# A graph network on one core: last edges looked up in a column of copied node rows, the dense moments spread over more turns, and more state gathers at a seam of the tail

## What is computed

```python
    def _L0_gnn_ref(x, edge_index, edge_bias, Wq, bq, Wk, bk, Wv, bv, Wo, bo):
...
        attn = jnp.einsum('ehd,ehd->eh', q_i, k_j) * scale + edge_bias
        seg_max = jax.ops.segment_max(attn, col, num_segments=N)
...
        out = jax.ops.segment_sum(weighted_v, col, num_segments=N)
...
    def _L1_gnn_ref(x, edge_index, edge_type, edge_emb_W, msg_W, msg_b, upd_W, upd_b, ln_g, ln_b):
...
        m = jax.nn.relu(m_in @ msg_W.T + msg_b)
        agg = jax.ops.segment_sum(m, dst, num_segments=x.shape[0])
...
    def _L3_gnn_ref(x, hyperedge_index, hyperedge_weight, W1, b1, gamma, beta, W2, b2):
...
        h = _hconv(x, W1, b1, node_idx, edge_idx, hyperedge_weight)
        mu = h.mean(axis=0)
        var = h.var(axis=0)
        h = gamma * (h - mu) * jax.lax.rsqrt(var + EPS) + beta
        return _hconv(h, W2, b2, node_idx, edge_idx, hyperedge_weight)
```

## Time and profile before

| | us |
|---|---|
| median of 3 runs | 2510.71 (2508.42 to 2510.8) |
| the profiled execution | 2507.46, of which the span from first to last instruction is 2505.7 |
| GpSimd busy | 1776.4 (71% of the span), 1419 instructions |
| VectorE busy | 1579.2 (63%) |
| TensorE busy | 1393.9 (56%) |
| ScalarE busy | 861.4 (34%) |
| mean granted TensorE clock | 0.772 of full speed |

### The profile page before, as it was taken

One profiled execution on the slowest core, in us unless ns is written; L12 is line 12 of the kernel. 1 busy time (PEld: TensorE's weight loads), 2 busy tenths in 40 slices (PEclk: granted clock), 3 DMA queues, 4 the chain that ended last, 5 costly groups with the idle time before them and its releaser, 6 DMA issues. The chain is left out here.

```text
span 2505.7 us, 21855 instructions
## 1 busy us (share of the span) xinstructions
PE 1393.9 (56%) x4580; PEld 725.9 (29%) x4580; DVE 1579.2 (63%) x4917; ACT 861.4 (34%) x1813; POOL 1776.4 (71%) x1419
## 2 busy tenths in 40 slices
PE   6778488888546666547888366354555640011121
PEld 1444244444313333213433244122223330001110
DVE  8889378878727989949899454243444464534443
ACT  0111156667515767735877211011112320000000
POOL 5774677777078888148787587788757878777887
PEclk8899699999768887768999687677777865555555
DMA  1111244444254566344666577567796863323331
GB/s 25 25 33 41 76 110 123 123 123 113 57 113 115 142 162 152 100 99 105 145 147 137 121 203 200 138 171 194 158 228 163 245 181 81 86 63 72 72 72 43
DMA packets 358128, 297.94 MB, mean 119 GB/s; under 512 B 110941, under 2 KB 312428, under 8 KB 357981
## 3 DMA queue, kind: packets, MB, share of 16 engines
q1 hardware_dynamic: 260397, 225.43, 33.4%
q0 software_dynamic: 97600, 71.11, 14.7%
HBM read 199.75 MB, written 96.70 MB: 118 GB/s over the span
## 5 line engine op out<-in xcount | busy, mean ns | idle before, releaser
L2219 DVE TENSOR_TENSOR_SCAN tl_S<-tl_same,tl_S,tl_pX 128x500 f32<-128x500 bf16 x96 | 120.3, 1253 | 317.6 <-issue 219.1
L2108 PE MATMUL tl_pX<-k_ident,tl_ga 125*128 125x125 f32 x400 | 84.6, 349 | 421.1 <-DMA tl_ga<-table_TE,k_s_idxE 321.8
L481 POOL DMA_INDIRECT tl_ga<-table_TE,k_s_idxE x200 | 243.0, 1215 | 63.4 <-issue 58.5
L2108 PEld LDWEIGHTS tl_pX<-k_ident,tl_ga 125*128 125x128 f32 x400 | 57.6, 178 | 437.0 <-DMA tl_ga<-table_TE,k_s_idxE 331.4
L481 POOL DMA_INDIRECT ms_ga<-table_T,k_idxS x100 | 143.4, 1434 | 36.1 <-issue 29.6
L481 POOL DMA_INDIRECT tl_ga<-table_TH,k_send x100 | 123.1, 1231 | 51.7 <-issue 51.1
L1288 PE MATMUL tl_pCon<-dr_BC,dn_cT 128*128 128x512 f32 x196 | 130.6, 754 | 51.2 <-DVE dr_o L1307 21.6
L283 POOL DMA_INDIRECT table_ptab<-k_ef,ix_scatI x100 | 124.8, 1248 | 47.9 <-issue 47.9
L481 POOL DMA_INDIRECT at_ga<-x,k_src x100 | 126.5, 1265 | 44.7 <-issue 27.3
L481 POOL DMA_INDIRECT at_gb<-xw,at_dstI x100 | 128.9, 1289 | 35.5 <-issue 29.0
L481 POOL DMA_INDIRECT eq_ga<-table_T,k_idxS x100 | 126.1, 1261 | 35.0 <-issue 30.0
(11 more groups left out here) (469 smaller groups left out, 4363.9 us busy)
## 6 DMA issues: line engine op xcount, KB each, us to landing
dr_x<-x SPq DMA_DIRECT2D x97, 256.0 KB
result<-dr_o SPq DMA_DIRECT2D x97, 256.0 KB
dm_xT<-xT SPq DMA_DIRECT2D x32, 768.0 KB
tl_fac<-table_dinv SPq DMA_DIRECT2D x50, 250.0 KB
table_T<-at_y SPq DMA_DIRECT2D x50, 224.0 KB
table_T<-ms_y SPq DMA_DIRECT2D x50, 224.0 KB
table_T<-eq_y SPq DMA_DIRECT2D x50, 224.0 KB
table_TE<-tl_y SPq DMA_DIRECT2D x50, 224.0 KB
```

The source lines that it names most:

```text
L481: nc.gpsimd.indirect_dma_start(out=buf[:, k, :], out_offset=None, in_=table, in_offset=bass.IndirectOffsetOnAxis(ap=index[:, CT * c + k:CT ...
L2108: last = nc.tensor.transpose(pX[j % 2][:, k * TP:(k + 1) * TP], ga[j % RG][:, k, :], K["ident"][0:TP, 0:TP])
L2219: nc.vector.tensor_tensor_scan(S[i][:], same[j % RM][:], pX[i][:, 0:CE], 0.0 if j % NC == 0 else S[1 - i][:, CE - 1:CE], ALU.mult, ALU.add ...
```

## The change

Six edits in one step.

1. **A table of node rows takes the place of `ptab`.** The input `xw` gets `E` in its column 129. SP copies the whole of it, 50000 rows of 132 numbers (26.4 MB), to a table `XW` in HBM, in 5 pieces, where it copied 195.3 KB. The 100 scatters of last edges write into column 129 of `XW`, and wait for the whole copy.
2. **No lookups.** Attention gathers its source rows from `XW` in place of `x` (528 bytes a row in place of 512), so the last edge comes with the row; `biased` copies it to `K["pq"]`. The 100 gathers of `pq` in index, attention and message phases go, and with them the message phase's `source_rows` (three small vector instructions a turn). One `source_rows` over all chunks stands at the end of attention.
3. **Moments in attention**: one group a turn and two in two turns of eight, in place of three in three turns of four (`AT_QUADS`); 3 supers, 24 turns, in place of 5 supers in 20. Squares come in three turns of eight.
4. **Moments with messages**: three groups in each of 24 turns (8 supers), transposes and keeping of one super beside the first groups of the next, with two PSUM banks.
5. **Records**: 13 chunks with messages (every second turn), 12 in the equivariant phase, in place of 6 and 19.
6. **The tail's seam**: 8 chunks of state gathers (`WIDE_SEAM`) after the second pass and 13 between its chunks, in place of 4 and 17. In the second half of the second pass one dense group a turn in place of two; the 12 groups that this leaves over (`dense_seam`) stand between the second and the third pass.

```diff
             for name in ("ident", "identb", "heads", "cols"):
                 sp.dma_start(K[name][:], g[name]).then_inc(s_in, 16)
-            sp.dma_start(T["ptab"].rearrange("(a b) c -> a (b c)", a=16), g["ptab0"].rearrange("(a b) c -> a (b c)", a=16)).then_inc(s_tab, 16)
+            for i in range(PIECES):
+                n = N // PIECES
+                sp.dma_start(T["XW"][n * i * DW:n * (i + 1) * DW, :].rearrange("(a b) o -> a (b o)", a=400),
+                             g["xw"][n * i:n * (i + 1), :].rearrange("(a b) c -> a (b c)", a=400)).then_inc(s_tab, 16)
...
-            pool.wait_ge(s_tab, 16)
+            pool.wait_ge(s_tab, 16 * PIECES)
             pool.wait_ge(s_ends_idx, 1)
             for t in range(NT):
                 nc.gpsimd.indirect_dma_start(
-                    out=T["ptab"], out_offset=bass.IndirectOffsetOnAxis(ap=scatI[:, t:t + 1], axis=0),
-                    in_=K["ef"][:, t:t + 1], in_offset=None, bounds_check=N - 1, oob_is_err=False).then_inc(s_scat, 16)
+                    out=T["XW"], out_offset=bass.IndirectOffsetOnAxis(ap=scatI[:, t:t + 1], axis=0),
+                    in_=K["ef"][:, t:t + 1], in_offset=None, bounds_check=N * DW - 1, oob_is_err=False).then_inc(s_scat, 16)
             pool.wait_ge(s_scat, 16 * NT)
-            for t in range(CT * PQ):
-                nc.gpsimd.indirect_dma_start(out=K["pq"][:, t:t + 1], out_offset=None, in_=T["ptab"],
-                                             in_offset=bass.IndirectOffsetOnAxis(ap=src[:, t:t + 1], axis=0)).then_inc(s_gat, 16)
...
-                gathers(pool, s_ga[c % RA], K["src"], c, g["x"], ga[c % RA])
+                gathers(pool, s_ga[c % RA], K["src"], c, T["XW"].rearrange("(n c) o -> n (c o)", c=DW), ga[c % RA])
...
-                    if s < MA:
-                        dn.moments(pe, s)
+                    if s < 8 * AT_SUPERS:
+                        dn.moments(pe, s // 8, range(AT_QUADS[s % 8], AT_QUADS[s % 8 + 1]))
+                        if s % 8 == 7:
+                            dn.turn_moments(pe, s // 8)
                     out(s)
...
-                nc.vector.tensor_tensor(z[c % 3][:, CT:2 * CT, :], ga[c % RA][:], bc(bo, CT), ALU.add).then_inc(s_z2, 1)
+                nc.vector.tensor_copy(K["pq"][:, CT * c:CT * c + CT], ga[c % RA][:, :, D + 1])
+                nc.vector.tensor_tensor(z[c % 3][:, CT:2 * CT, :], ga[c % RA][:, :, 0:D], bc(bo, CT), ALU.add).then_inc(s_z2, 1)
...
-                if live(s + 3 + PQA):
-                    last_edges(s + 3 + PQA)
-                if 0 <= s - 14 < SLOTS:
-                    records(s - 14)
+                if s >= 0 and s % 2 == 0 and s // 2 < SLOTS:
+                    records(s // 2)
...
-                    dn.moments(pe, MA + s)
+                    if s > 0 and s % 3 == 0:
+                        dn.turn_moments(pe, AT_SUPERS + s // 3 - 1)
+                    if dn.ms_part(s) is not None:
+                        dn.moments(pe, AT_SUPERS + s // 3, range(3 * (s % 3), 3 * (s % 3) + 3))
...
+AT_QUADS = (0, 2, 3, 4, 5, 6, 7, 9, 9)
+AT_PARTS = (0, 2, 5)
...
             for c in range(NC):
                 fetch(J_NODE + c)
-                if c + SEAM < NC - SEAM:
+                if c + SEAM < NC - WIDE_SEAM:
                     keep_states(c + SEAM)
-            for c in range(NC - SEAM, NC):
+            for c in range(NC - WIDE_SEAM, NC):
                 keep_states(c)
             stored(pool, J_EDGE)
...
                 if t == J_EDGE:
                     batch_norm()
+                    for d in dense_seam():
+                        dn.combine(dve, d)
```

More of the change, by code:

```diff
@@ L43 @@
 RING = 4
-PQ = 6
-PQA = 10
-SLOTS = 6
+SLOTS = 13
+PIECES = 5
 class Chain:
@@ L1121, in flatten, with moments @@
-    def flatten(self, act, j):
-        h = j // 4
-        if j >= MT or j % 4 < 3:
-            return
+    def moments(self, pe, h, quads):
+        nc, pS = self.nc, self.bank_of(h)
+        count = min(PACK, DQ - PACK * h)
+        for k in quads:
+            if k >= count:
+                return
+            n = 3 * h + k // 3
+            a, b = self.span(n)
+            u = 512 * (k % 3)
+            w = min(512, b - a - u)
+            if k % 3 == 0:
+                pe.wait_ge(self.s_xT[n % 2], 16 * (n // 2 + 1))
+                pe.wait_ge(self.s_z2, n + 1)
+            if k == 0:
+                need(pe, self.s_kept, h + 1 - len(self.pS))
+            at = PW - NV - NV * k
+            nc.tensor.matmul(pS[0:PW, 0:w], self.Vx[:, at:at + PW], self.xT[:, n % 2, u:u + w], start=k == 0, stop=False)
+            last = nc.tensor.matmul(pS[0:PW, 0:w], self.Vz[:, at:at + PW], self.z2[:, n % 2, u:u + w], start=False, stop=k == count - 1)
+            if k % 3 == 2 or k == count - 1:
+                last.then_inc(self.s_mom, 1)
@@ L1126, in flatten, with turn_moments @@
+    def turn_moments(self, pe, h):
+        pe.wait_ge(self.s_flat, h + 1)
+        for i in range(4):
+            last = self.nc.tensor.transpose(self.bank_of(h)[:, i * PW:(i + 1) * PW], self.flat[:, i * 128:(i + 1) * 128], self.K["ident"][0:PW, 0:PW])
+        last.then_inc(self.s_mT, 1)
+    def flatten(self, act, h):
         act.wait_ge(self.s_mom, 3 * h + 3)
         need(act, self.s_mT, h)
-        self.nc.scalar.activation(self.flat[:], self.pS[0:PW, :], ACT.Identity, bias=self.off[:]).then_inc(self.s_flat, 1)
@@ L1332, in message_phase @@
         pA, pM, pO, pR = (a.ps(n, [128, 512]) for n in ("pA", "pM", "pO", "pR"))
-        dn.pS = a.ps("pS", [128, 512])
-        miss = a.sb("miss", [TP, CT])
-        s_pq = [a.sem(f"last_edges{i}") for i in range(2)]
-        s_idx, s_miss, s_rec = a.sem("source_rows"), a.sem("miss"), a.sem("records")
+        dn.pS = [a.ps(f"pS{i}", [128, 512]) for i in range(2)]
+        s_rec = a.sem("records")
         (s_w, s_eps, s_kind, s_tw, s_tA, s_xs, s_oneh, s_psM, s_m, s_S, s_psO,
@@ L1901, in _, with first, dense_seam @@
                 dn.coefficients(dve, s)
+SEAM, WIDE_SEAM, SEAM_ROWS = 4, 8, 12
+KEPT = 2 * NC - SEAM - WIDE_SEAM
 def dense_turn(t):
-    first = [min(DQ, u if u < NC else min(2 * u - NC, u + NC)) for u in (t, t + 1)]
-    return range(first[0], first[1])
+    def first(u):
+        if u <= NC:
+            return u
+        if u <= KEPT:
+            return 2 * u - NC
+        return min(DQ, u + KEPT - NC + (SEAM_ROWS if u > 2 * NC else 0))
+    return range(first(t) + (SEAM_ROWS if t == 2 * NC else 0), first(t + 1))
+def dense_seam():
+    n = dense_turn(2 * NC).start
+    return range(n - SEAM_ROWS, n)
 def tail_phase(nc, g, K, T, dn):
@@ L2145, in _ @@
                     rows(job(t - 1))
+                if t == J_EDGE:
+                    for d in dense_seam():
+                        dn.expand(pe, d)
                 if job(t) is not None:
@@ L2197, in _ @@
                     act.wait_ge(s_bn, 2)
+                    for d in dense_seam():
+                        dn.turned(act, d)
                 if job(t) is not None and t >= J_NODE:
@@ L2355, in layout @@
         oC[r, 0:U] = w["L2_gnn_w_lin2_s"][U:2 * U]
-    ptab = np.full((N, 1), E, f)
     xw = np.zeros((N, DW), f)
     xw[:, 0:D] = w["x"]
+    xw[:, D + 1] = E
     xw[0:NH, D] = w["L3_gnn_hyperedge_weight"]
```

135 lines of the change are left out of this document (45 added, 90 removed).

## The result

| | before | changed |
|---|---|---|
| median, us | 2509.57 (2507.94 to 2510.8) | 2451.14 (2449.57 to 2452.97) |
| span of the profiled execution | 2505.7 | 2451.1 |

The kernel was run once more beside two of the experiments (`c_changed`).

A forecast was written before the change was run, and what follows sets the result against it. Each phase has its own limit: VectorE in index and equivariant, TensorE in attention's full turns, GpSimd's gathers in early messages and the tail. Terms 58 - 43 - 28 - 1 - 21 = -35 gave 2475 us, range 2432 to 2514.

The forecast's parts named there:

- Index, the copy: Index phase: the table's copy at 250 GB/s takes 106 us and delays the first rank to 128; +58 us.
- rival A: Index phase: the copy streams at 400 GB/s, 66 us, ranks 18 us late; total 2436 us; chance 0.20.
- Rivals B and C: Copy at 210 GB/s, 2495 us, chance 0.24; copy under 187 GB/s, slower than before, 2545 us at 150 GB/s, chance 0.12.
- Rival D: Index phase: the loads overtake the copy, so the phase gains 35 us; total 2452 us; chance 0.04.
- Attention: Attention phase: spread moments fill TensorE's hole and keep its clock up, 13.1 us a turn; -43 us.
- Rival E: Attention's turns don't shorten by the clock, 13.9 us each, 19 us less gained; 2494 us; chance 0.04 alone.
- Messages: Message phase: without lookups VectorE bounds it from the first turn, 12.7 us a turn; -28 us.
- the ramp: Start of the message phase: third chunk's gathers stand behind eight lookups fewer, 12 us, of which 5 counted.
- Equivariant: Equivariant phase: 28 scatters, 42 us of GpSimd, leave a phase that VectorE bounds; -1 us.
- Tail: Tail: GpSimd's 21.5 us pause at the seam between second and third pass goes; -21 us.

The follow-up runs named there:

- e3_short_runs: The changed kernel with the same 26.4 MB copied in runs of 13200 bytes in place of 55000; 2456.99 us, ratio 0.9778.
- e1_loads_first: The changed kernel with the index phase's first three loads issued by SyncE ahead of the table's copy, not behind it; 2446.83 us, ratio 0.9745.
- e6_lookups: The changed kernel with the old distribution of records and 60 unread lookups put back in the message phase; 2488.64 us, ratio 0.9932.
- e4_old_seam: The changed kernel with the tail's seam and dense groups of the kernel before; 2472.53 us, ratio 0.9852.
- e2_own_queue: The changed kernel with the table's copy on ScalarE's queue, after the first three loads have landed, other loads staying on SyncE's; 2450.79 us, ratio 0.9763.
- e8_six_ahead: The changed kernel with six `srcb` buffers in place of two and a load behind each of the copy's first pieces; 2444.35 us, ratio 0.9743.

## Why the prediction was right, and where not

- **Index, the copy: the step that failed.** Forecast +58, measured +31.5; 26.5 us off, where the whole sum was 20 off by the spans (35 forecast, 54.6 measured). The mechanism was right: the loads stood behind the copy, the first rank started 32.6 us late at 102.9, the scatters ended ahead of the ranks (255.4 and 288.7). The rate was wrong: 322 GB/s and 82 us, between the forecast's 250 (95 to 115 us) and rival A's 400 (66 us), at a rate to which no named case belonged; the total stayed in the range because the range was wide. The row I priced it by, 16 packets in 0.8 us, was too short to tell a rate, and `e3_short_runs` shows that the packet's size was not what made it slow either. The second row I leaned on, 257 GB/s at a share of 0.92, was of mixed small transfers and says nothing of a copy's ceiling; the seam still shows 253 at 0.93. Rivals B and C, which needed 210 GB/s or less, are out. The Trainium skill's 207 to 214 GB/s ("DMA: Bandwidth & Descriptors", Latency and other measured facts) does not hold for this copy of contiguous pieces; the measurement decides.
- **Rival D** (the loads overtake): false on the same queue, where the first rank waited for the copy's end, and in `e1_loads_first` the third load did. Its 2452 us is nevertheless the named time nearest to the 2451.14 measured: the time alone would have picked the wrong mechanism.
- **Attention**: a turn of 13.1 us forecast, (665.7 - 349.9)/24 = 13.16 measured, clock 0.98. The phase gained 38.6 and not 43, since its way in, from the first gather to the first `at_o`, is 52.1 us in place of 48.9 and its way out 0.3 longer. Rival E (no gain by the clock, 13.9) is out. (In the turns of eight, five have one group, two have two and the last has none, so the groups are nine, not the ten that "one group a turn and two in two turns" makes.)
- **Messages**: -28 forecast, -29.4 measured, and `e6_lookups` confirms the cause. The agreement is in part luck, two sizes that were wrong in opposite ways. The mean of 12.58 us a turn against 12.7 holds a first turn of 3.0; the other 23 took 13.0 each, which is a gain of 17 us and not 23. The way from the phase's first gather to the second `ms_mean` shrank from 39.1 to 26.9 us, 12 where I had counted 5 for the ramp. And the lookups cost 39.2 us in `e6_lookups`, more than the 28.
- **Equivariant**: -1 forecast, +0.9 measured, nothing that can be told from no change.
- **Tail**: -21 forecast, -19.0 measured; the first gather of `TH` had 0.31 us before it, as forecast. The 2 us between are not shown to be the moved dense rows: with the old seam and the old dense turns `e4_old_seam` has a tail 3.1 us longer than the kernel before (1106.8 against 1103.7), which I can't explain.

## What to carry to other kernels

Before a long copy goes on a queue, list what must land while it runs: put all of that ahead of it, in enough buffers, and cut each load so that it spreads over all DMA engines. Another queue alone did not help here: the engines took one packet of each queue in turn, and every small row ahead of the load waited for a run of 55 KB. Price a large copy by a large transfer of the same kind, or keep the range wide; a burst of under a microsecond gave 250 GB/s where the copy made 322. Filler work on TensorE is worth most where it is spread, one piece into each hole: here its place was worth 32.5 us, and the rest of what was edited in the phase 6.1. Ask of a table that saves lookups what it costs to make: here about what it saved.

## What the runs showed of the hardware that I had not expected

- A table copied within HBM ran at about 320 GB/s with the DMA engines 0.97 busy, in runs of 55 KB (82 us for 26.4 MB); in runs of 13.2 KB it was 5% slower (86 us, 312 to 326 GB/s).
- Two queues at work on the same engines took turns packet by packet, whatever the size: rows of 250 bytes, ten at a time, every 2.5 to 2.9 us, between runs of 55 KB that take 2.7 us (`e2_own_queue`). The load behind them did not move in 28 us.
- A load of 125 rows between pieces of a copy left about 5 engines behind by some 20 us (`e8_six_ahead`: first scatter at 125.8 against 105 expected); as 112 and 13 rows, two behind each of the first two pieces, it did not (110.3).
- SyncE stood for 39.70 us in the issue of two small loads behind the copy.
